# Selective scan: projections in two steps with a detour through DRAM, six decay buffers, splitting and skip term on TensorE

## What is computed

```
x_dbl = einsum('bkdl,kcd->bkcl', xs, x_proj_weight)          # 6 + 16 + 16 rows
dts, Bs, Cs = x_dbl[:, :, :R], x_dbl[:, :, R:R+N], x_dbl[:, :, R+N:]
dt = softplus(einsum('bkrl,kdr->bkdl', dts, dt_projs_weight) + dt_projs_bias)
h = h * exp(dt * A) + (dt * u) * B                            # for each channel and state
y = sum over states of h * C
ys = ys + Ds * u ; the four directions are summed in image order
```

## Time and profile before

| | us |
|---|---|
| median of three runs | 3111.86 (3110.11 to 3114.77) |
| the profiled execution | 3110.97, of which span 3108.9 |
| VectorE busy | 2223.0 (72%) |
| TensorE busy | 2521.1 (81%), mean granted clock 0.834 |
| GpSimd busy | 1311.6 (42%) |
| ScalarE busy | 1424.7 (46%) |

### The profile page before, as it was taken

How to read it: one execution, slowest core, us unless ns; L and a number is a source line. 1 busy time by engine, 2 the same in 40 slices (tenths; PEclk the granted TensorE clock), 3 DMA queues, 4 the chain that set the end, 5 groups by cost and what they waited for, 6 DMA issues and landing times. The chain is left out here.

```text
span 3108.9 us, 33979 instructions
## 1 busy us (share of the span) xinstructions
PE 2521.1 (81%) x9156; PEld 920.0 (30%) x9156; DVE 2223.0 (72%) x3030; ACT 1424.7 (46%) x1949; POOL 1311.6 (42%) x677
## 2 busy tenths in 40 slices
PE   4677677776677766776668689999999889999999
PEld 2111111111111111111124123232232246666766
DVE  4999999999999998999755688787878631111112
ACT  3444544445444444444456147676767522222221
POOL 1788878787788877788751100000000200000000
PEclk9777767777677777777758689999999889999999
DMA  3555555555555555555512603131313400000000
GB/s 88 144 167 165 160 152 166 154 155 159 157 168 162 166 146 152 160 152 163 152 47 80 104 2 43 23 42 24 42 23 42 87 1 6 5 5 5 5 5 10
DMA packets 101755, 286.76 MB, mean 92 GB/s; under 512 B 14878, under 2 KB 19137, under 8 KB 101569
## 3 DMA queue, kind: packets, MB, share of 16 engines
q1 hardware_dynamic: 100506, 284.94, 35.1%
q10 hardware_dynamic: 1102, 0.19, 0.0%
HBM read 239.66 MB, written 25.88 MB: 85 GB/s over the span
## 5 line engine op out<-in xcount | busy, mean ns | idle before, releaser
L528 POOL TENSOR_TENSOR hs<-hs,bc 128x1024 f32<-128x1024 f32 x384 | 900.4, 2355 | 224.9 <-DVE hs L614 224.2
L501 ACT ACTIVATE decay<-decay,a_neg 128x1024 f32<-128x1024 f32 x384 | 440.4, 1148 | 666.2 <-DMA decay<-dt_rows 652.3
L425 PE MATMUL psU<-stack,spread_sel 96*128 96x512 bf16 x768 | 361.1, 487 | 425.0 <-DVE hs L614 346.3
L1446 DVE TENSOR_REDUCE mx<-ps 128x1 f32<-128x512 f32 x864 | 539.3, 682 | 117.7 <-PE ps L1285 112.4
L558 DVE TENSOR_TENSOR psU<-psU,bc 128x512 f32<-128x512 f32 x768 | 514.4, 673 | 25.9 <-issue 13.4
L1421 ACT ACTIVATE P<-ps 128x512 f32<-128x512 f32 x768 | 417.6, 599 | 249.3 <-PE ps L1297 225.2
L614 DVE TENSOR_TENSOR_SCAN hs<-decay,psU 128x512 f32<-128x512 f32 x384 | 464.7, 1210 | 72.6 <-PE psY L387 52.4
L614 DVE TENSOR_TENSOR_SCAN hs<-decay,hs,psU 128x512 f32<-128x512 f32 x384 | 487.5, 1269 | 1.1
L387 PE MATMUL psY<-hs,state_sel 128*32 128x512 f32 x1572 | 401.5, 855 | 23.2 <-DVE Y L571 11.2
L1719 DVE SCALAR_TENSOR_TENSOR acc<-psE,gate,acc 128x192 f32<-128x192 f32 x128 | 53.4, 417 | 448.5 <-PE psE L1619 445.5
L1285 PE MATMUL ps<-ks,qs 96*128 96x512 bf16 x864 | 345.0, 404 | 34.8 <-DMA ks<-qk_parts 24.2
(11 more groups left out here) (237 smaller groups left out, 2280.3 us busy)
## 6 DMA issues: line engine op xcount, KB each, us to landing
decay<-dt_rows SPq DMA_DIRECT2D x388, 512.0 KB
stack<-parts SPq DMA_DIRECT2D x297, 64.0 KB, 5.5
dt_rows<-dt SPq DMA_DIRECT2D x33, 384.0 KB, 7.1
qs<-qk_parts SPq DMA_DIRECT2D x90, 128.0 KB, 6.7
ks<-qk_parts SPq DMA_DIRECT2D x90, 128.0 KB, 7.2
qk_parts<-qparts SPq DMA_DIRECT2D x16, 576.0 KB, 3.7
w<-in_L_ffn_w_dram SPq DMA_DIRECT2D x8, 576.0 KB, 9.9
X<-in_x_dram SPq DMA_DIRECT2D x4, 768.0 KB, 9.7
```

The lines of the kernel that those rows point to most:

```text
L425: pe.matmul(psU[:, q % UR, :], s.spread_sel[:, gg, :], stack[:, ui % 2, j, CH * pos:CH * pos + CH], start=True, stop=True).then_inc(dtu_sp ...
L501: nc.scalar.activation(decay[:, t % DR, :], decay[:, t % DR, :], ACT.Exp, scale=s.a_neg[:, col:col + 1]).then_inc(decay_ready, 1)
L528: pool.tensor_tensor(h, h, bc[:, 2 * p + r, 1, :], ALU.mult).then_inc(hc_ready, 1)
L1446: v.reduce_max(mx[:, slot, u:u + 1], ps1[:, (slot * MAXES + u) % R, :], AX.X).then_inc(max_done, 1)
```

## The change

1. **Two-step projections.** PE projects x to the 38 rows of `x_dbl` only (`inputs`, weights `w_xd`, 4 times in an image, not 32), ACT copies them to `xd`. The step comes from `xd` by a second small matmul (`steps`). B and C go to DRAM (`bc_rows`) and are loaded from there, repeated 8 times on the partitions: two loads of 512 KB for each of the four directions of an image (`load_bc`). No product of weight matrices is made in `prepare`.
2. **Six decay buffers** instead of four, and eight `hs` buffers instead of six; the step is kept in four DRAM slots instead of two.
3. **Splitting on PE.** The remainders `dtu - hi` and `dtu - hi - mid` are made by PE (`remainder`: an fp32 matmul with the identity, bf16 matmuls with its negative) and rounded by ACT. POOL's two subtractions go. All three parts go to DRAM (`dtu_parts`) and come back as three transfers of 192 KB.
4. **Order and skip term.** Units are ordered by channel half first. PE adds Ds*u (`skip`) and reads `hs` transposed for column directions, so all four directions of a half add up in `psY`; ACT copies it to `Y` once in four units. DVE keeps only increments and recurrences. There is no `xt`: PE and POOL read `X` with a stride of 32 elements for column directions.

```diff
-                for q in range(2 * K):
-                    bank, at = 6 + q // K, 0
-                    m = pe.transpose(ps[0:R, bank, at + HC * (q % K):at + HC * (q % K) + HC], wdt_rows[:, q, :],
-                                     s.ident[0:HC, 0:HC])
-                m.then_inc(pe_wdt, 1)
-                pe.wait_ge(wdt_turned, 1)
-                for k in range(K):
-                    for f in range(2):
-                        m = pe.matmul(ps[0:HC, 2 + k, D * f:D * f + D], wx[0:R, k, HC * f:HC * f + HC],
-                                      wdt[:, k, :], start=True, stop=True)
...
-        HR, DR, UR = 6, 4, 4
-        xt = sb("xt", [HC, 2, L])
+        HR, DR, UR = 8, 6, 4
+        xd = sb("xd", [128, 2, L])
...
-            p, f, r = ui // 4, ui // 2 % 2, ui % 2
-            return p, f, r, p + 2 * r
+            f, p, r = ui // 4, ui // 2 % 2, ui % 2
+            return f, p, r, p + 2 * r
...
+                def inputs(out, nb, p, c):
+                    for h in range(2):
+                        m = pe.matmul(out, s.w_xd[:, p, h, :], turned(s.X[:, nb, h, :], p)[:, 16 * c:16 * c + 16, :],
+                                      start=(h == 0), stop=(h == 1))
+                    m.then_inc(xd_proj, 1)
+
+                def steps(nu, c):
+                    f, p, r, k = order(nu)
+                    pe.matmul(psP[0:HC, c, :], s.w_dt[BLK * r:BLK * r + R, p, HC * f:HC * f + HC],
+                              xd[BLK * r:BLK * r + R, p, CH * c:CH * c + CH], start=True, stop=True).then_inc(z_proj, 1)
+
+                def remainder(c, known, ready):
+                    cs = slice(CH * c, CH * c + CH)
+                    m = pe.matmul(psP[0:HC, c, :], s.ident[0:HC, 0:HC], dtu[:, cs], start=True, stop=False)
+                    for i in range(known):
+                        m = pe.matmul(psP[0:HC, c, :], s.minus_bf[:], parts[:, i, cs], start=False, stop=(i == known - 1))
+                    m.then_inc(ready, 1)
...
+                        h = h.rearrange("p (w h) -> p h w", h=HH) if p else h.rearrange("p (h w) -> p h w", h=HH)
...
+                def take(b, f, last):
+
+                    act.wait_ge(summed, last + SUM0)
+                    nc.scalar.copy(s.Y[:, b, f, :], psY[0:HC, :, :].rearrange("p c l -> p (c l)")).then_inc(y_taken, 1)
...
-                            if t == 2:
-                                pool.wait_ge(hi_ready, n + 2)
-                                pool.tensor_tensor(rest[:], dtu[:], parts[:, 0, :], ALU.subtract).then_inc(rest_ready, 1)
...
-                            if q % 6 == 0:
-
-                                v.wait_ge(summed, n * SUB + (SUB + q // 6 + START))
...
+                                if (t - HR) % 3 == 0:
+
+                                    v.wait_ge(summed, n * SUB + ((t - HR) // 3 + 1 + SUM0))
...
-                            if q == 8 and r == 0:
-                                take(n - 1, b if ui else (b + (NB - 1)) % NB, (ui - 1) % UNITS)
...
+                def load_bc(slot, which=(0, 1)):
+                    p, r = slot // 2, slot % 2
+                    for i in which:
+                        at = BLK * r + N * i
+                        src = s.bc_dram[p, at:at + N, :].unsqueeze(0).broadcast_to([DD, N, L])
+                        sp.dma_start(bc[:, slot, i, :], src).then_inc(bc_landed[slot], 16)
...
-                            if t in (4, 5, 7):
-                                part = (4, 5, 7).index(t)
-                                sp.wait_ge((hi_ready, mid_ready, lo_ready)[part], n + 2)
-                                stack_up(part, (ui + 1) % 2)
+                            if t == 2 and ui in (5, 6, 7, 0):
+                                sp.wait_ge(hc_ready, n * TILES + (TILES + START))
+                                load_bc((ui - 5) % UNITS, (0,))
+                            if t == 4 and ui in (5, 6, 7, 0):
+                                load_bc((ui - 5) % UNITS, (1,))
+                            if t == 4 and ui in XD_UNITS:
+                                sp.wait_ge(xd_ready, b * 4 + (2 * XD_UNITS[ui] + 6))
+                                keep_xd(XD_UNITS[ui])
+                            if t == 5:
+                                sp.wait_ge(mid_ready, n * 2 + 4)
+                                keep_parts((ui + 1) % 2, 0, 2, hm_stored)
+                            if t == 6:
+                                sp.wait_ge(lo_ready, n * 2 + 4)
+                                keep_parts((ui + 1) % 2, 2, 1, lo_stored)
+                            if t == 7:
+                                sp.wait_ge(hm_stored, n * 16 + 32)
+                                sp.sem_inc(rows_kept, 1)
+                                sp.wait_ge(lo_stored, n * 16 + 32)
+                                stack_up((ui + 1) % 2)
```

More of the change, by code:

```diff
@@ L266, in _ @@
                 own.wait()
+                v.wait_ge(gp, 3)
+                for f in range(2):
+                    own(v.tensor_scalar(s.d_diag[:, f, :], s.ident[0:HC, 0:HC], s.d_sum[:, f:f + 1], None, ALU.mult))
+                own(v.tensor_scalar(s.minus_bf[:], s.ident[0:HC, 0:HC], -1.0, None, ALU.mult))
+                own.wait()
+        nc.clear_and_free_semaphores(sems)
+        nc.all_engine_barrier()
 def scan(nc, w, s):
@@ L346, in _ @@
                 pe.sem_inc(scan_done, S0)
-                pe.sem_inc(summed, 2 + START)
+                pe.sem_inc(summed, SUM0 - 2)
                 for first in (y_taken, hc_ready):
                     pe.sem_inc(first, START)
[L351 to L366, removed]
@@ new lines, in z_end, with part @@
+                def z_end(n1):
+                    act.wait_ge(z_taken, n1 * 2 + 2)
+                    nc.scalar.activation(soft[:], soft[:], ACT.Exp, scale=-1.0).then_inc(exp_own, 1)
+                    act.wait_ge(exp_own, n1 + 1)
+                    nc.scalar.activation(soft[:], soft[:], ACT.Ln, bias=s.one[0:HC, :]).then_inc(log_ready, 1)
+                def part(i, n1, c, rest, ready):
+                    act.wait_ge(rest, n1 * 2 + (c + 1))
+                    nc.scalar.copy(parts[:, i, CH * c:CH * c + CH], psP[0:HC, c, :]).then_inc(ready, 1)
@@ new lines, in _ @@
+                for c in range(2):
+                    z_half(0, 0, c)
+                z_end(0)
+                act.wait_ge(dtu_ready, 1)
+                nc.scalar.copy(parts[:, 0, :], dtu[:]).then_inc(hi_ready, 1)
+                for c in range(2):
+                    part(1, 0, c, rest_ready, mid_ready)
+                for c in range(2):
+                    part(2, 0, c, tail_ready, lo_ready)
+                act.wait_ge(dt_stored, 16)
+                for c in range(2):
+                    z_half(1, 1, c)
@@ new lines, in _ @@
+                            if t == 4:
+                                act.wait_ge(hm_stored, n * 16 + 16)
+                                act.wait_ge(lo_stored, n * 16 + 16)
+                                act.wait_ge(dtu_ready, n + 2)
+                                nc.scalar.copy(parts[:, 0, :], dtu[:]).then_inc(hi_ready, 1)
+                            if t == 4 and ui % 4 == 0:
+                                take(b if ui else (b + (NB - 1)) % NB, 1 - f, n * SUB)
+                            if t == 6:
+                                for c in range(2):
+                                    part(1, n + 1, c, rest_ready, mid_ready)
@@ L514, in _ @@
+                take(NB - 1, 1, NB * UNITS * SUB)
             @block.gpsimd
@@ L619, in _, with keep_dt @@
             @block.sync
             def _(sp):
-                def store(par):
-                    sp.dma_start(s.dt_dram[par], dt[:]).then_inc(dt_stored, 16)
-                def stack_up(part, slot):
-                    for j in range(NBLK):
-                        sp.dma_start(stack[BLK * part:BLK * part + BLK, slot, j, :],
-                                     parts[BLK * j:BLK * j + BLK, part, :]).then_inc(stacked[slot], 16)
-                def load(par, t):
+                def keep_dt(slot):
+                    sp.dma_start(s.dt_dram[slot], dt[:]).then_inc(dt_stored, 16)
@@ new lines, in keep_parts, with stack_up @@
+                def keep_parts(slot, first, n, stored):
+                    sp.dma_start(s.parts_dram[slot, first:first + n].rearrange("a p l -> p a l"),
+                                 parts[:, first:first + n, :]).then_inc(stored, 16)
+                def stack_up(slot):
+                    for part in range(QPART):
+                        sp.dma_start(stack[BLK * part:BLK * part + BLK, slot, :, :],
+                                     s.parts_dram[slot, part].rearrange("(j r) l -> r j l", j=NBLK)).then_inc(stacked[slot], 16)
@@ L634, in _ @@
+                for p in range(2):
+                    sp.wait_ge(xd_ready, 2 * p + 2)
+                    keep_xd(p)
+                sp.wait_ge(xd_stored, 32)
+                load_bc(0)
                 sp.wait_ge(dt_ready, 1)
[L635 removed]
+                keep_dt(0)
```

(1 more changed line is left out.)

350 lines of the change are left out of this document (165 added, 185 removed).

## The result

The changed kernel took 3221.49 us (median of four runs), the kernel before 3113.32 us beside it on the same chip: a ratio of 1.0342, 95% interval 1.0317 to 1.0366, so 3.4% slower. The profiled execution took 3222.61 us, 111.6 more than that of before. Medians are over all executions of a kernel, ratios leave out those in which the chip ran in its slower state: one of four of the changed kernel, two of four of "Four decay buffers" (its profiled one among them) and one of four of "Straight sums".

A forecast was written before the change was run, and what follows sets the result against it. Transfers were taken to set the pace in most units, just ahead of VectorE. 3111.0 us + 145 (transfers) + 16 (start) = 3272 us; eight-in-ten range 3080 to 3430 us, likeliest case 3190 to 3362 us.

The forecast's parts named there:

- 0.55 is a full DMA: Scan: a DMA share of 0.55 is what full looks like, as decay loads run on 8 of 16 engines.
- In most units the transfers set the pace: Scan of the kernel before: transfers, just ahead of VectorE, make units 45.8 us, 4.0 over VectorE's necessary work.
- Transfers, +145 us: Scan units: 8.45 MB instead of 7.27 at 168 GB/s, 50.3 us a unit, adding 145 us.
- Worth nothing while that holds: VectorE in the scan: 26 us of takings and 52 us of `psY` waits saved, hidden beside the longer transfers.
- The change adds, per unit: one load of B or C: Scan transfers: eight loads per image over eight units, 0.524 MB more in each unit.
- costs nothing on top of the transfers: SP's wait at the eighth tile until the parts land in DRAM: covered by six decay buffers, nothing added.
- Start, +16: Before the first increment: 5.37 MB instead of 2.69 to move, adding 16 us, bounds 8 and 30.
- TensorE's stride, nothing: Sums in column units read `hs` at a stride of 128 bytes: taken as no added time.
- rival B: TensorE becomes the bound in column units: 3400 us at 2.3 ns an element, 3619 at 3.2; chance 14%.
- GpSimd's strided product: GpSimd's product with x at a stride may double, 2.3 us more in half of the units; there is room.
- A: Rival: VectorE sets the pace, transfers keep up; 129 us less, 16 us for the start, 2998 us; chance 20%.
- C: Rival: the transfer rate rises, but not enough: 180 GB/s, 46.9 us a unit, 3165 us; chance 11%.

The follow-up runs named there:

- Four decay buffers: The changed kernel with four decay buffers instead of six: 3227.17 us, ratio 1.0297 to the kernel before.
- Straight sums: The changed kernel, but TensorE reads `hs` without a stride in the sums of column units too: 3197.17 us, ratio 1.0339 to the kernel before.

## Why the prediction was right, and where it was off

**What bounds the kernel: right for the changed kernel, not for the one before.** That 0.55 is a full DMA was a reading of one trace. By the rule of the Trainium skill (DMA: Bandwidth & Descriptors, "Why a DMA increments its semaphore by 16 and not by 1") the loads had 8 of 16 engines. Two experiments bear it out: with 16 rows to a load the share rose to 0.79 and the time fell, by 113 us after and by 31 us before the change.

"In most units the transfers set the pace" was wrong for the kernel before: without that hold it gained 31 us, not 129. The rows already said who takes the 129 us: takings 26 and idle time before increments 26, waits for `psY` 52 and for decay 20, 124 together, of which only the 20 are plainly the transfers'. The wait for `psY` did not shrink without the hold either (58 us). A share that stays flat shows that loads are always in flight, not that they hold VectorE.

**Transfers, +145 us: the number was close, in part by luck.** Forecast were 50.3 us a unit at 168 GB/s; measured 47.8 at 177, my upper bound. The rate rose by 12%, from 159 to 178 GB/s, about half by share (0.54 to 0.57), half by quicker packets. Against a kernel without the added loads and the detour they cost 134 to 141 us. That is near 145, but from other terms: the sum set units too slow (50.3 us) against units of 45.8 us that it took for the transfers' own. In truth 159 GB/s was no limit of the queue: without the added bytes the same loads ran at 168 GB/s and a unit took 43.9 us. So the step that failed is the one on VectorE's gains, "Worth nothing while that holds": the rest of the change, costed at nothing, gave 29 us, 57 in the units less a later start. The two bounds were so close that neither held all units. Which part of it gives the 29 us (the eight `hs` buffers, the taking of the sums, the order) wasn't tried one by one; the decay buffers alone are not it.

**"The change adds, per unit: one load of B or C": failed in part.** The sum spread these loads evenly over the units. The reloads come in pairs in four units of eight. Two of those four and the unit after them take 49 to 60 us, the others 41 to 48, many of them near VectorE's 41.8; what a long one loses, a short one can't give back. Spreading them gave 28 to 39 us.

**The detour "costs nothing on top of the transfers".** SP's wait is 260 us long, and taking 183 of them away gave 5 to 13 us, not told from nothing, so this much is right. Taking the whole detour away gave 82 to 92 us, where its bytes at 177 GB/s (0.590 / 0.177 = 3.3 us a unit) are worth 107 as an estimate. So its bytes are enough to account for the cost, though no run took the bytes away and left the round trip. Where I was wrong is whom it makes wait: not decay, whose buffers are refilled behind it, but the stack (193 us against 11), since the stores and their return stand in the same queue behind the decay loads.

**Start, +16:** the first increment came at 95.84 us, not 91: +20. The first unit and the end of the scan, which I did not cost apart, gave another 26 us.

**TensorE's stride, nothing:** no cost to the kernel that could be told, and rival B falls, though more by the price in the trace than by the experiment. That price, 2.24 us for a group at either clock against 1.06 or 1.93, is under both figures taken from ScalarE and VectorE: 2.24 / 2048 is 1.1 ns an element, little over half of the 1.9 from which it would have decided; eight such groups and the 19 us of other work are 37 us a unit, under the 47.8 measured.

**GpSimd's strided product** took 2614 ns in the mean over both kinds of units, 2354 before: hidden, as costed, and far less than double. With the stride it took 2842 to 2889 ns, without it 2339 to 2451.

```profile
L555 POOL TENSOR_TENSOR dtu<-dt,X 96x1024 f32<-96x1024 f32 x32 | 83.7, 2614 | 0.0
```

**Rivals.** A needed 187 GB/s to come out even and got 177; the loads over 16 rows show it from the other side, 195 GB/s and a ratio of 0.9993. That kernel stores the step twice, so 8.84 MB a unit, and 8.84 / 195 = 45.3 us is the unit at which A was to come out even (45.4 measured). C, at 180 GB/s and 3165 us, was nearest in rate; of the 56 us by which it falls short, 0.9 us a unit are 29 and the first unit and the end of the scan 26. (Under B, the 3400 us for 2.3 ns an element should have been 3375: 19 + 8 x 4.7 = 56.7 us, 16 x 6.4 = 102 us over 3272.)

## What to carry to other kernels

A DMA share that stays at the same level in short and in long stretches was these loads' full mark here, though it was 0.55. Whether it holds the kernel is another question: add up what the pacing engine waited for, by cause, before giving all of a unit's excess to one bound (124 of 129 us had names, and only 20 of them were the transfers'). Lay out the source so that a broadcast load has 16 rows outermost before buffers are added: that gave 113 us here, while four buffers or six made no difference that could be told. Count the bytes for each unit, not the mean: two loads more in four units of eight cost 28 to 39 us over the same loads spread out. Savings against the same bound don't add up (92 and 113 gave 137) when the next bound, here VectorE, is near. And taking away a wait is worth little if the data then wait elsewhere: without SP's wait the return took 15.3 us to land, not 3.7 to 5.0, in the unit shown.

## What the runs showed of the hardware

Decay loads over 16 rows raised the share by 39% (0.57 to 0.79) and the rate by 10% (178 to 195 GB/s): each packet took longer, a packet of 4 KB 264 ns in the mean of 150 to 1500 us where it took 203. In the kernel before the share went from 0.54 to 0.65, the rate from 159 to 170 GB/s and such a packet from 219 to 243 ns. Here more engines at work did not give their sum; why packets took longer was not found.

With the same share a unit of the kernel before moved 137 or 177 GB/s, and two neighbouring units of the changed one 152 and 191 at 0.55 and 0.56. Why packets were slower in some units stays open for both kernels.

TensorE's fp32 sums with a stride of 128 bytes took 2.2 to 2.3 us a group of three at either clock, 78 groups at 2.4 GHz and 53 at 1.2, where groups without the stride took 1.06 or 1.93. So the read, and not the clock, set their time. GpSimd's product with one input at that stride took 2.84 to 2.89 us against 2.34 to 2.45.
